# Two graph convolutions: rows gathered as three bf16 parts, one bf16 product per step into a fixed PSUM place, parts joined and added by the vector engine

## What is computed

```python
def gcn_conv(x, src, dst, W, b, n_nodes):
    ones = jnp.ones(src.shape[0], dtype=x.dtype)
    deg = jax.ops.segment_sum(ones, dst, num_segments=n_nodes)
    dinv = jnp.where(deg > 0, jax.lax.rsqrt(jnp.maximum(deg, 1.0)), 0.0)
    norm = dinv[src] * dinv[dst]
    h = x @ W
    msg = h[src] * norm[:, None]
    out = jax.ops.segment_sum(msg, dst, num_segments=n_nodes)
    return out + b
h = jax.nn.relu(gcn_conv(x, src, dst, W1, b1, n))
return gcn_conv(h, src, dst, W2, b2, n)
...
x = _layernorm(x + _L3_gnn_ref(x, edge_index, L3_gnn_W1, L3_gnn_b1, L3_gnn_W2, L3_gnn_b2), axis=-1)
```

## Time and profile before

| | us |
|---|---|
| runs of the kernel | 16833.16, 16849.05, 16851.1 (median 16849.05) |
| the profiled execution | 16738.64, span 16736.7 |
| convolution 0, first gather to the end of the sums | 11720.64 to about 14134 |
| convolution 1, likewise | 14209.33 to about 16623 |
| busy in the whole span | PE 9065.6, DVE 6730.9, ACT 2109.6, POOL 10470.8 |

### The profile page before, as it was taken

One profiled execution on the slowest core, in us unless ns is written; L12 is line 12 of the kernel. 1 busy time (PEld: TensorE's weight loads), 2 busy tenths in 40 slices (PEclk: granted clock), 3 DMA queues, 4 the chain that ended last, 5 costly groups with the idle time before them and its releaser, 6 DMA issues.

```text
span 16736.7 us, 184234 instructions
## 1 busy us (share of the span) xinstructions
PE 9065.6 (54%) x49642; PEld 8394.0 (50%) x49643; DVE 6730.9 (40%) x11202; ACT 2109.6 (13%) x3404; POOL 10470.8 (63%) x8750
## 2 busy tenths in 40 slices
PE   4777777745555555555454555897333334333333
PEld 4777777734444544444444444786233333333333
DVE  4444444444444448988333333555111112111112
ACT  0111111111211213333000000333000000000000
POOL 2888888836666667775566666000666665666664
PEclk7666666666666665555666666665555555555555
DMA  4333333333333332221122122111111111111111
GB/s 79 18 18 18 18 18 18 18 83 101 104 102 103 105 101 75 71 71 53 44 46 46 45 46 45 48 49 44 26 23 23 23 23 26 23 23 23 23 23 24
DMA packets 857869, 780.45 MB, mean 47 GB/s; under 512 B 631552, under 2 KB 637908, under 8 KB 855509
## 3 DMA queue, kind: packets, MB, share of 16 engines
q0 software_dynamic: 455488, 343.42, 14.7%
q1 hardware_dynamic: 402351, 436.64, 8.0%
HBM read 526.17 MB, written 253.20 MB: 47 GB/s over the span
## 4 chain that ended last, share of the span: by engine, by line
another core or an unknown queue 23%; PE 21%; issue 19%; DVE 16%; POOL 8%; DMA 7%; DVEq 4%; SPq 1%; ACT 0%; POOLq 0%; ACTq 0%
PE ps L973 9%; POOL lane_tab L602 8%; DMA lane_tab<-rows,idx 6%; PE ps L944 3%; PE ps L945 3%; DVE buf_a L397 2%; DVE acc_w L1335 2%; DVE buf_b L1359 2%; DVE tmp_c L1422 2%; DVE mx L1428 1%; DVE buf_a L1416 1%; PE ps L969 1%; DVE tab L397 1%; PE ps L1015 1%
## 5 line engine op out<-in xcount | busy, mean ns | idle before, releaser
L616 POOL DMA_INDIRECT buf_b<-gcn_tab,idx x1664 | 1634.1, 982 | 2338.8 <-issue 1830.5
L602 POOL DMA_INDIRECT lane_tab<-rows,idx x1664 | 2598.1, 1561 | 786.3 <-issue 785.4
L969 PE MATMUL ps<-ident_b,zero_b 128*128 128x260 bf16 (+1 forms) x1664 | 506.9, 407 | 3882.2 <-DVE buf_a L397 2847.2
L616 POOL DMA_INDIRECT aux<-att_tab,idx x1664 | 1587.7, 954 | 1018.9 <-issue 502.7
L1335 DVE TENSOR_TENSOR acc_w<-acc_w,ps 128x520 f32 (+1 forms) x832 | 573.7, 690 | 4019.9 <-remote 2863.3
L969 PEld LDWEIGHTS ps<-ident_b,zero_b 128*128 128x128 bf16 x1664 | 194.9, 147 | 3936.0 <-DVE buf_a L397 2699.3
L616 POOL DMA_INDIRECT buf_c<-gcn_tab,idx x1664 | 1674.9, 1007 | 507.3 <-issue 500.0
L973 PEld LDWEIGHTS ps<-buf_c,buf_a 128*128 128x128 f32 x6656 | 1417.5, 323 | 181.7 <-issue 167.8
L1006 PE MATMUL ps<-ident,buf_a 128*128 128x128 f32 x3328 | 915.9, 363 | 1060.6 <-DVE buf_a L1416 575.2
L973 PE MATMUL ps<-buf_c,buf_a 128*128 128x65 f32 (+1 forms) x6656 | 1449.4, 408 | 70.2 <-issue 70.2
L616 POOL DMA_INDIRECT buf_b<-src_tab,idx x832 | 909.9, 1094 | 668.2 <-issue 259.0
(11 more groups left out here) (233 smaller groups left out, 18428.7 us busy)
## 6 DMA issues: line engine op xcount, KB each, us to landing
y_stash<-buf_c SPq DMA_DIRECT2D x208, 512.0 KB
tab<-y_stash SPq DMA_DIRECT2D x208, 512.0 KB, 3.3
h_stash<-aux SPq DMA_DIRECT2D x208, 264.0 KB
aux<-in_edge_attr_dram SPq DMA_DIRECT2D x1696, 32.0 KB
rows<-h_stash SPq DMA_DIRECT2D x104, 264.0 KB, 2.8
tab<-h_stash SPq DMA_DIRECT2D x104, 264.0 KB, 2.8
lane_tab<-rows,idx POOLq DMA_INDIRECT x1664
aux<-att_tab,idx POOLq DMA_INDIRECT x1664
```

The lines of the kernel that those rows point to most:

```text
L602: pool.indirect_dma_start(lane_tab[k][:, :], bass.IndirectOffsetOnAxis(ap=idx[:, b, u:u + 1], axis=0), rows[:, b, u, 0:D1], None, compute_ ...
L616: pool.indirect_dma_start(to[q][:, u, :], None, table[:, :], bass.IndirectOffsetOnAxis(ap=idx[:, q, u:u + 1], axis=0)).then_inc(rows_in[q] ...
L969: pe.matmul(ps[:, bank + c, :].rearrange("p (k f) -> p k f", f=P)[:, :, 0:n], zero_b[:, :], bc(ident_b[:, 0:n].unsqueeze(1), [P, 4, n]), s ...
```

## The change

- The table is bf16 with 192 numbers a row (384 bytes): each float32 number is kept as three bf16 parts, whose sum gives it back. Before each convolution DVE scales in two halves into `aux` (L1563 for convolution 0), and per half ACT rounds to part 0, DVE subtracts it (L1561), ACT rounds the rest to part 1, DVE subtracts, ACT rounds part 2. SP stores the halves one by one.
- `one_hot` (L407 now) writes bf16 into `g_hot`. The product of a step is one bf16 product of 192 columns into a half bank of its own (L1007). Nothing is zeroed, PE loads no registers, and steps don't add up in PSUM.
- DVE per group: it loads 8 window numbers instead of one, waits for the sums, frees the ring place, sums the three parts of all 8 steps from PSUM into `buf_d` in one reduction (L1589), frees the banks, and adds the 8 steps one after another into `acc_w` at their windows (L1595), each waiting for the one before.
- At the end of a convolution DVE waits for the last add.

The core of the diff:

```diff
         aux_flat = aux[:, :, :].rearrange("p a b -> p (a b)")
         ob = aux_flat[:, 0:G * P].bitcast(BF16).rearrange("p (b u f) -> p b u f", b=2, u=G)
         ot_b = buf_d[:, 0, :, :].rearrange("p u f -> p (u f)").bitcast(BF16).rearrange("p (b u f) -> p b u f", b=2, u=G)
-        g_rows = [buf_b[:, k, :, 0:D] for k in range(2)] + [buf_c[:, k, :, 0:D] for k in range(2)]
+
+        def split_rows(buf, k):
+            return buf[:, k, :, :].rearrange("p u f -> p (u f)").bitcast(BF16)[:, 0:G * D3].rearrange("p (u f) -> p u f", f=D3)
+
+        g_rows = [split_rows(buf_b, k) for k in range(2)] + [split_rows(buf_c, k) for k in range(2)]
+        g_hot = buf_a[:, 0, :, :].rearrange("p u f -> p (u f)").bitcast(BF16).rearrange("p (b u f) -> p b u f", b=2, u=G)
+        g_sum = [buf_d[:, k, :, 0:D] for k in range(2)]
         att_ring = aux_flat[:, 2 * G * P:2 * G * P + RING * G * D2].rearrange("p (q u f) -> p q u f", q=RING, u=G)
         att_rows = [att_ring[:, q, :, :] for q in range(RING)]
         sq = aux_flat[:, G * P:3 * G * P].rearrange("p (b u f) -> p b u f", b=2, u=G)
...
                                  h_stash[bass.ds(g, 1), :, :].rearrange("a p f -> (a p) f")).then_inc(h_in[q], 16)
-            for k, (ready, stored) in enumerate(((s.gcn_in0, s.gcn_stored0), (s.gcn_in1, s.gcn_stored1))):
-                sp.wait_ge(ready, 1)
-                sp.dma_start(gcn_tab[k].rearrange("(p w) f -> p w f", p=P), tab_d).then_inc(stored, 16)
+            for k in range(2):
+                for h, (start, end) in enumerate(OUT_PARTS):
+                    sp.wait_ge(s.split_kept, k * 2 + h + 1)
+                    sp.dma_start(gcn_tab[k].rearrange("(p w) f -> p w f", p=P)[:, start:end, :],
+                                 tab_b[:, start:end, :, :].rearrange("p w r f -> p w (r f)")).then_inc(s.gcn_stored, 16)
             for k, (start, end) in enumerate(OUT_PARTS):
...
             act.activation(scratch, scratch, ACT.Exp).then_inc(s.elu_out, 1)
             std(3)
             std(4)
+
+            def split_parts(conv):
+                for part in range(3):
+                    for h, (start, end) in enumerate(OUT_PARTS):
+                        act.wait_ge(s.split_rest, conv * 6 + 2 * part + h + 1)
+                        act.activation(tab_b[:, start:end, part, :], rest_d[:, start:end, :],
+                                       ACT.Copy).then_inc(s.split_part if part < 2 else s.split_kept, 1)
+
+            split_parts(0)
             act.wait_ge(s.l2_indices, RING * (TURNS + 1))
             indices(s.g0_indices)
             with act.Fori(0, TURNS) as i:
...
                                      start=False, stop=True, skip_group_check=True)
                 return last
-            def aggregate(n, left_ready, conv, free, done):
+            def aggregate(left_ready, conv, free, done):
                 with pe.Fori(0, TURNS) as i:
                     for q in range(RING):
                         g = i * RING + q
                         pe.wait_ge(left_ready, g + 1)
                         rows_landed(pe, i, q, conv)
                         pe.wait_ge(free, g + 1)
-                        add_group(buf_a[:, q % 2, :, :], g_rows[q], g, 2 * (q % 2), n).then_inc(done, 1)
+                        for u in range(G):
+                            last = pe.matmul(ps[:, 4 * (q % 2) + u // 2, (u % 2) * 256:(u % 2) * 256 + D3], g_hot[:, q % 2, u, :], g_rows[q][:, u, :],
+                                             start=True, stop=True)
+                        last.then_inc(done, 1)
             with pe.Fori(0, ITER // 2) as i:
...
             dinv_bc = bc(mx[:, :].unsqueeze(2), [P, W, D])
-            link(dve.tensor_tensor(tab_d, x_n[:, :, :], dinv_bc, ALU.mult))
-            dve.sem_inc(s.gcn_in0, 1)
+            def split(conv, scaled):
+                for start, end in OUT_PARTS:
+                    scaled(rest_d[:, start:end, :], start, end).then_inc(s.split_rest, 1)
+                for part in range(2):
+                    for h, (start, end) in enumerate(OUT_PARTS):
+                        rest = rest_d[:, start:end, :]
+                        dve.wait_ge(s.split_rest, conv * 6 + 2 * part + h + 1)
+                        dve.wait_ge(s.split_part, conv * 4 + 2 * part + h + 1)
+                        dve.tensor_tensor(rest, rest, tab_b[:, start:end, part, :], ALU.subtract).then_inc(s.split_rest, 1)
+
+            split(0, lambda to, start, end: dve.tensor_tensor(to, x_n[:, start:end, :], dinv_bc[:, start:end, :], ALU.mult))
             def to_acc(c, k, conv):
                 for k0, k1 in ((0, 4), (4, 7)):
...
                                              bc(bias3[:, conv:conv + 1, :], [P, k1 - k0, D]), ALU.add)
                 last.then_inc(s.node_evacuated, 1)
-            def gcn(o, outs, accfree, gfree, order):
+            def parts(bank):
+                return ps[:, bank:bank + 4, :].rearrange("p c (k x) -> p (c k) x", x=256)[:, :, 0:D3].rearrange("p u (r f) -> p u f r", r=3)
+
+            def gcn(conv, o, outs, accfree, gfree, order):
                 dve.memset(acc_w[:, :, :], 0.0).then_inc(order, 1)
                 dve.sem_inc(accfree, 2)
                 dve.sem_inc(gfree, RING)
...
                     for b in range(2):
                         g = i * 2 + b
                         dve.wait_ge(outs, g + 1)
-                        one_hot(dve, buf_a[:, b, :, :], g).then_inc(o, 1)
+                        one_hot(dve, g_hot[:, b, :, :], g).then_inc(o, 1)
                     for b in range(2):
                         g = i * 2 + b
-                        w0 = load1(mybir.EngineType.DVE, win_s, g, W - 1)
+                        ws = load8(mybir.EngineType.DVE, win_s, g, W - 1)
                         dve.wait_ge(outs, g + 3)
                         dve.sem_inc(gfree, 1)
-                        add_windows(g, 2 * b, w0, D, order)
-                        dve.wait_ge(order, g + 2)
+                        dve.tensor_reduce(g_sum[b], parts(4 * b), AX.X, ALU.add).then_inc(s.split_joined, 1)
+                        dve.wait_ge(s.split_joined, g + (conv * 2 * ITER + 1))
                         dve.sem_inc(accfree, 1)
-
-            gcn(s.g0_hot, s.g0_sums, s.g0_bank_free, s.g0_rows_used, s.g0_added)
-            dve.wait_ge(s.gcn_stored0, 16)
+                        for u in range(G):
+                            a = acc_w[:, bass.ds(ws[u], 1), 0:D].rearrange("p a f -> p (a f)")
+                            dve.wait_ge(order, g * G + (u + 1))
+                            dve.tensor_tensor(a, a, g_sum[b][:, u, :], ALU.add).then_inc(order, 1)
+
+            gcn(0, s.g0_hot, s.g0_sums, s.g0_bank_free, s.g0_rows_used, s.g0_added)
+            dve.wait_ge(s.g0_added, S + 1)
+            dve.wait_ge(s.gcn_stored, 32)
             link(dve.tensor_tensor(tab_d, sums_d, dinv_bc, ALU.mult))
             dve.sem_inc(s.node_in, 1)
             chunks(3 * CHUNKS, lambda c, k: to_acc(c, k, 0))
-            link(dve.scalar_tensor_tensor(tab_d, sums_d, 0.0, dinv_bc, ALU.max, ALU.mult))
-            dve.sem_inc(s.gcn_in1, 1)
-            gcn(s.g1_hot, s.g1_sums, s.g1_bank_free, s.g1_rows_used, s.g1_added)
-            dve.wait_ge(s.gcn_stored1, 16)
+            split(1, lambda to, start, end: dve.scalar_tensor_tensor(to, sums_d[:, start:end, :], 0.0, dinv_bc[:, start:end, :], ALU.max, ALU.mult))
+            gcn(1, s.g1_hot, s.g1_sums, s.g1_bank_free, s.g1_rows_used, s.g1_added)
+            dve.wait_ge(s.g1_added, S + 1)
+            dve.wait_ge(s.gcn_stored, 64)
             link(dve.tensor_tensor(tab_d, sums_d, dinv_bc, ALU.mult))
             dve.sem_inc(s.node_in, 1)
             chunks(4 * CHUNKS, lambda c, k: to_acc(c, k, 1))
```

## The result

The changed kernel took 16977.5 us (median; 16974.87 to 16995.98) beside 16842.08 for the kernel before (16833.16 to 16851.1): ratio 1.0078, 95% interval 1.0066 to 1.0091. It is slower by some 135 us. I had forecast 16522. The time lies inside the range I gave, between the rival in which the wait for a ring place shrinks (16886) and the one in which it stays whole (17073), and on the other side of no change from the forecast.

The account below looks back on a forecast made before the run. The prediction took POOL's gather issue plus a 4.7 us wait a turn for a ring place as the bound. Turns -364, preparation +34 and ends +3 gave -327 us, from 16849 to 16522, range 16380 to 17050.

Parts of the forecast that it names:

- the rival in which the wait for a ring place shrinks: Convolution turns: POOL still waits 3.8 us in place of 4.96, adds cost 1.2; +37 us, 16886; chance 0.14.
- Where the bound is: Convolution turns: POOL's own gather issue plus 4.7 us a turn waiting for a ring place, 46.26 us in all.
- PE's lateness by the number of its instructions, so the wait goes: Convolutions: fewer PE products let sums come in time, removing POOL's wait, 4.7 us a turn over 104 turns.
- the chain of eight adds becomes the bound: DVE's joins: adds 1.2 us apart instead of 0.35 make the turn 55 us; some +950, 17800; chance 0.05.
- the wait stays whole and the adds come on top: Convolution turns: no wait goes and adds stretch gathers by 1.8 us a turn; +224, 17073; chance 0.17.
- The adds' stretch of the gathers: POOL's gathers beside DVE's small adds: lengthened by 1.2 us a turn, between 0 and 2.4.
- The rows' size: POOL's gathers: rows of 384 bytes instead of 256 cost nothing, taken as 0.
- The preparation: Before each convolution: splitting and storing the table puts the first gather at 33.6 us, 17 more each, 34 for both.
- The single figures: Instruction times: reduction 1.8 us, a small add 0.23 and 0.35 apart, PE's products 1.8 us a group.
- The end of a convolution: After the last gather: sums sooner but joins longer, about 2 us more each, 3 taken for both.
- Sum: Whole kernel: -364 for the turns, +34 preparation, +3 ends, together -327 us.
- The range: Whole kernel: 16380 to 17050 us with chance 0.80, holding the forecast and the lower half of the whole-wait rival.

Follow-up runs that it names:

- j3: Changed kernel with one PSUM add a group, each gather fetching 64 rows instead of 128, products over 64 partitions: 16640.89 us, 0.9955 of the kernel before, slow chip.
- i1: Changed kernel with one PSUM add a group of the first part alone, no reduction: 16627.91 us, 0.9961 of the kernel before, slow chip.
- j1: i1 plus 20 empty DVE instructions a group that only raise an unused semaphore: 16829.46 us, 1.0065 of the kernel before, slow chip.
- j2: Changed kernel with its eight adds at fixed windows, without register load and address work: 16691.15 us, 0.9984 of the kernel before, slow chip.
- e1: Changed kernel with one add of 128x512 from SBUF in place of the eight adds: 15693.17 us, 1.0138 of the kernel before, quick chip.
- f3: Changed kernel with PE adding steps of one window up in PSUM, one reduction and one 128x512 add: 15474.0 us, 0.9997 of the kernel before, quick chip.

## Why the prediction was wrong, step by step

- **Where the bound is: right in its reading, not as a sum.** The turn is POOL's issue plus a wait for a ring place, on the slow chip. But the two can't be changed one by one: in j3 POOL's issue got shorter and the wait longer by as much. On quick chips the kernel before is POOL's 40.0 + 1.8 us a turn, with 9.4 us of waits in all.
- **PE's lateness by the number of its instructions, so the wait goes (4.7 us a turn, 488 us): the step that failed**, in two ways. First, in size: with PE's part of the change alone (i1) the waits only fell from 515.6 to 421.3 us, though PE's records in a turn fell from 195 to 75. Second, and decisive, I applied it to PE and not to DVE. I counted PE's records, from 72 to 32 products, and did not count DVE's instructions, which grew from 17 to 63 in the loop over two groups. I had taken the spacing of the adds (0.28 us of one column, so 0.35) from a stretch of the earlier trace rows at one of POOL's pauses. That is the right figure for a quick stretch (0.37 measured) and six to eight times too small for a slow one (2.1 to 2.8). The price is what j1 and j2 show: 170 to 200 us for 80 more instructions a turn, and 160 back for 40 fewer.
- **The rival** "the chain of eight adds becomes the bound" had the mechanism nearest to this one: it decides from 0.8 us apart, and I gave it 0.05. In the changed kernel a quarter of the adds of a group come over 0.8 us behind the one before (695 of 2912), and the mean spacing is 0.82 us. Its cause, the chain, isn't what makes them slow: on the quick chip the same chain runs at 0.37 throughout.
- **The rival** "the wait stays whole and the adds come on top" gave 17073 by 1.8 us of stretched gathers a turn. The mechanism was another: the gathers were not stretched (1643 and 1647 us busy, less than before), the wait itself grew from 4.96 to about 6 us a turn.
- **The adds' stretch of the gathers, 1.2 us a turn (0 to 2.4): wrong in sign for the whole.** The busy time of the gathers fell by 7 to 12 us a convolution on the slow chip and by 57 and 54 on the quick one (1669.28 to 1611.93 in convolution 0).
- **The rows' size, 0: right.** The median gather takes 0.944 us of 384 bytes and 0.947 of 256, on the quick chip 0.944 of either.
- **The preparation, 33.6 us to the first gather for 16.6: right**, 33.3.
- **The single figures: right.** Reduction 1.758 us (1.8), an add 0.226 (0.23), eight products 1.4 us (1.8, too much, but hidden).
- **The end of a convolution, 3 us in all: too small.** It was 19, because DVE is behind when the gathers end; on the quick chip, where it isn't, the two ends take 16.9 us together for 15.5.
- **Sum.** In place of -364 + 34 + 3 the profiled executions show +112 + 33 + 19 = +165, and the medians +135. The 30 us between them no run explains; the stages ahead of the change differ by more between the same two executions.
- **The range** held the time, as it reached to the rival. The chance of 0.60 for faster rested on a mechanism that I had described as unnamed and then given a law; i1 is what it was worth. That the change is faster on quick chips is no support for it: there was no wait to remove there, and the gain is one of shorter gathers that I had not foreseen.

## What to carry to other kernels

Where an engine is fed slowly beside another one's work, count its instructions, the register loads and address steps included, before counting its busy time: PE's work fell by two thirds here and the kernel got slower on the slow chips, where DVE's 46 more instructions for each two groups cost more than PE's fewer gave. Take a spacing from the same kind of stretch as the one that decides, at the end of a long run of gathers and not behind a pause. And if idle time is put down to nothing the profile can show, find out first whether it is there on every chip; this change is worth -0.5% on one kind and +0.8% on the other.

## What the runs showed of the hardware

**Slow instructions beside gathers, on some chips only.** While POOL issues indirect gathers without a break, the small instructions of DVE's queue take up to 1.4 us in place of 0.04, and some 4 us after it stops they run at full speed. The changed kernel on the slow chip of the result shows it, and j1 and j2 on another; on the two other slow chips ran only kernels with 44 and 50 of DVE's records a turn, and there PE's side alone was late. None of three quick chips shows either. Halving the packets doesn't lessen the waits; adding instructions to DVE makes them longer. The instructions aren't loaded anew in the loops: in the whole of the changed kernel's execution the two DMA queues of instructions move 15 packets each, on the slow chip as on the quick one. What resource it is stays open. All times here come from executions that carry the profiler's spans and clocks, so the runs can't exclude that the recording of instructions has a part in it.

**When DVE lengthens a gather.** A gather is held up if, about 0.12 us after it starts, DVE is within an instruction that reads two inputs from SBUF, and it then ends 0.82 us after that instruction, if that is later than its usual end. In the whole of e1, 619 of 3328 gathers meet the condition and 615 of them take over 0.97 us; of the other 2709 none does. DVE and POOL there:

```profile
13614.28 0.69 DVE L1594 TENSOR_TENSOR acc_w<-acc_w,buf_d 128x512 f32 x1 [0.25 <-DVE buf_d L1589]
13614.89 2.35 DVE L407 TENSOR_TENSOR buf_a<-iota,dst_s 128x1024 bf16<-128x1024 f32 x2
...
13614.45 1.34 POOL L628 DMA_INDIRECT buf_b<-gcn_tab,idx  x1 [0.30 <-issue]
13616.09 1.97 POOL L628 DMA_INDIRECT buf_b<-gcn_tab,idx  x1 [0.30 <-issue]
```

The add ends at 13614.97 and the first gather at 13615.79; the one-hots end at 13617.24 and the second gather at 13618.06, both 0.82 later. (The two one-hots follow each other without a gap and count as one.) The price thus isn't DVE's busy time but how its instructions fall against the gathers' 1.25 us. That explains what no cost by size could: one add of 128x512 from SBUF took 1762 us of gathers in e1 and the same add 1649 in f3, eight small ones 1612 in the changed kernel, and the kernel before 1669. It is the whole of the change's gain on a quick chip: 57 and 54 us of shorter gathers less 33 us of preparation and a few at the end are the 75. The Trainium skill, "SBUF — State Buffer", section "Who interferes with whom", says that such an instruction contends with GpSimd's reads but infers that it leaves descriptor generation alone; the rows show a gather held by it, for one short part near its start. A gather also reads its 128 indices from `idx` in SBUF, so this may be the contention of reads that the page states; no run here separates the two.
